# A transformer layer: shift rows turned by VectorE, row maxima made ten steps ahead

## The reference

```python
q = (x @ wq).reshape(B, S, 16, 16); k, v = (x @ wk), (x @ wv)   # 4 key/value heads
q = q * cos + rotate_half(q) * sin                              # the same for k
scores = einsum('bqkgd,bskd->bkgqs', q, k) / sqrt(16)
x = layernorm(x + einsum('bkgqs,bskd->bqkgd', softmax(scores), v) @ wo)
h = silu(x @ Wg.T) * (x @ Wu.T)                                 # W = (int - 128) * scale
x = layernorm(x + h @ Wd.T)
```

## Time and profile before

| | |
|---|---|
| median of 3 runs | 936.12 us (935.14 to 936.33) |
| span of the profiled execution, slowest core | 932.5 us |
| mean granted TensorE clock | 0.988 |
| busy: PE / DVE / ACT / POOL | 98% / 81% / 77% / 27% |
| share of the chain that ended last: PE | 92% |
| row_max transpositions (line 1186) | 32, median 277 ns |
| shift DMAs (line 363) | 128, median 634 ns |

### The profile page before, as it was taken

One profiled execution on the slowest core, in us unless ns is written; L12 is line 12 of the kernel. 1 busy time (PEld: TensorE's weight loads), 2 busy tenths in 40 slices (PEclk: granted clock), 3 DMA queues, 4 the chain that ended last, 5 costly groups with the idle time before them and its releaser, 6 DMA issues.

```text
span 932.5 us, 15773 instructions
## 1 busy us (share of the span) xinstructions
PE 914.6 (98%) x5574; PEld 465.6 (50%) x5574; DVE 753.7 (81%) x1519; ACT 715.2 (77%) x932; POOL 249.5 (27%) x214
## 2 busy tenths in 40 slices
PE   9998999999999999999999999999999999999996
PEld 3323434343443434434344344434335888888885
DVE  5777999999999999999999999999973456655555
ACT  2456898989889988889988989898896555555564
POOL 7752565010010001001000100400101666656455
PEclk9997999999999999999999999999999999999998
DMA  7986433222133132223313133221110201101001
GB/s 258 281 227 189 96 90 84 72 69 52 43 75 80 43 66 59 51 65 70 72 42 75 46 63 70 69 51 43 32 52 15 70 24 46 46 23 46 24 24 47
DMA packets 50080, 68.78 MB, mean 74 GB/s; under 512 B 13520, under 2 KB 23760, under 8 KB 50000
## 3 DMA queue, kind: packets, MB, share of 16 engines
q1 hardware_dynamic: 49136, 64.61, 26.9%
q0 software_dynamic: 864, 3.15, 1.1%
HBM read 46.74 MB, written 16.25 MB: 68 GB/s over the span
## 4 chain that ended last, share of the span: by engine, by line
PE 92%; DVE 3%; ACT 2%; issue 1%; DMA 1%; SPq 1%; POOL 0%; POOLq 0%; DVEq 0%; ACTq 0%
PE pv_bank L1266 27%; PE ring_bank L1173 26%; PE pair_bank L1324 13%; PE pair_bank L1387 11%; PE pv_bank L1413 3%; PE ring_bank L1413 3%; PE ring_bank L1276 2%; PE pair_bank L1214 2%; ACT probs L1087 1%; PE ring_bank L1186 1%; PE ring_bank L1291 1%; PE pv_bank L1155 1%; PE ring_bank L1229 0%; DMA q_parts<-low 0%; DVE by_sin L727 0%
## 5 line engine op out<-in xcount | busy, mean ns | idle before, releaser
L1087 ACT ACTIVATE probs<-pair_bank 128x1024 f32<-128x1024 f32 x512 | 496.4, 1026 | 68.8 <-PE pair_bank L1324 67.6
L762 DVE TENSOR_REDUCE block_max<-ring_bank 128x1 f32<-128x512 f32 x732 | 468.8, 682 | 31.6 <-PE ring_bank L1173 23.7
L1173 PE MATMUL ring_bank<-k_max,q_sb 48*128 48x512 f32 x1003 | 314.8, 475 | 3.6 <-ACT above L1032 1.4
L1266 PE MATMUL pv_bank<-probs,v_all 128*32 128x512 f32 x2048 | 273.5, 606 | 0.6 <-ACT probs L1087 0.5
L1173 PEld LDWEIGHTS ring_bank<-k_max,q_sb 48*128 48x128 f32 x1003 | 136.5, 184 | 251.9 <-DVE block_max L762 127.4
L1324 PE MATMUL pair_bank<-q_sb,k_sb 50*128 50x512 f32 x1024 | 204.9, 416 | 0.9 <-ACT probs L1087 0.7
L619 POOL TENSOR_TENSOR attn<-attn,inv_rows 128x1024 f32<-128x1024 f32 x7 | 16.7, 2384 | 491.4 <-DMA inv_rows<-inv_d 491.4
L1324 PEld LDWEIGHTS pair_bank<-q_sb,k_sb 50*128 50x128 f32 x1024 | 101.2, 186 | 33.6 <-ACT probs L1087 15.1
L944 DVE SCALAR_TENSOR_TENSOR hid<-pair_bank,up_s,silu 128x512 f32<-128x512 f32 x63 | 47.1, 747 | 84.7 <-ACT silu L1134 84.7
L667 POOL TENSOR_TENSOR hid_l<-hid,hid_h 128x512 fp32r<-128x512 f32 x63 | 81.8, 1298 | 86.0 <-ACT hid_h L1113 85.3
L759 DVE CUSTOM_DVE_ANT_0 above<-ring_bank,above 128x512 f32<-128x512 f32 x137 | 94.4, 691 | 12.5 <-ACT above L1032 5.2
(11 more groups left out here) (140 smaller groups left out, 860.6 us busy)
## 6 DMA issues: line engine op xcount, KB each, us to landing
k_max<-k_parts SPq DMA_DIRECT2D x96, 96.0 KB, 3.5
q_sb<-q_parts SPq DMA_DIRECT2D x64, 128.0 KB, 3.4
k_sb<-k_parts SPq DMA_DIRECT2D x96, 64.0 KB, 2.3
attn<-xT SPq DMA_DIRECT2D x8, 512.0 KB, 5.1
q_parts<-high SPq DMA_DIRECT2D x16, 256.0 KB, 3.8
q_parts<-low SPq DMA_DIRECT2D x16, 256.0 KB, 4.1
q_sb<-q_parts SPq DMA_DIRECT2D x64, 64.0 KB, 3.5
attn<-pv_sb SPq DMA_DIRECT2D x128, 32.0 KB
```

Of the source, the lines that this page charges most:

```text
L762: dve.reduce_max(block_max[half % 2][:, col:col + 1], bank, axis=AX.X).then_inc(ring_used, 1)
L1087: act.activation(probs[t % 2][:, 2 * pr:2 * pr + 2, :], pair_bank[pr][:], ACT.Exp, scale=D ** -0.5).then_inc(probs_ready, 1)
L1173: pe.matmul(bank, q_sb[k][rows, i, qt * P:(qt + 1) * P], k_max[k // QH][rows, kind * CH:(kind + 1) * CH], start=True, stop=True).then_inc( ...
L1266: ins = pe.matmul(pv_bank[32 * j:32 * j + 2 * D, :], v_all[:, head, t, :], probs[t % 2][:, 2 * (j % 2) + j // 2, :], start=(t == 0), stop= ...
```

## The change

The turn from columns to rows goes from TensorE to VectorE. `row_max` is rounded where it lies, as 128x16 (`shift_high`), then the remainder is taken (`shift_low`), both into `shift_rows`, 128 partitions by 32 columns. `turn_shift` transposes this in four squares of 32x32: after it, partition 32 b + 16 o + c of `shift` holds part o of column c for the 32 queries of block b. TensorE's transposition and its ring bank go away; the three instructions stand behind the second, third and fourth block of a step.

Since each row of `q_sb` is now spread over four squares, `load_shift` issues eight DMAs, one for each part and square, each with 16 pieces of 32 numbers. It waits for a semaphore of its own, `shift_ready`.

`LEAD` goes from 12 to 10, so a half's last maxima are made in step 5 of the half before instead of step 3, and the three instructions stand in step 6 (`HIGH_AT`). For half 0 they stand behind blocks 2, 3 and 6 of the second half's early blocks. In the last pair the output projection's first part (`OUT_AT` = 6) waits for the last maxima.

```diff
-LEAD = 12
-SPLIT_AT = 5
+LEAD = 10
+HIGH_AT = 6
+OUT_AT = 6
...
-        shift = [sb(f"shift{c}", [G * QT, SHIFT, P], f32r, two) for c in range(2)]
+        shift_rows = [sb(f"shift_rows{c}", [P, SHIFT, G * QT], f32r, two) for c in range(2)]
+        shift = [sb(f"shift{c}", [P, SQ], fp32, two) for c in range(2)]
...
-            def load_shift(pair, k, split):
-                sp.wait_ge(*split)
-                for r in range(GROUPS):
-                    heads = G // GROUPS * QT
-                    for o in range(SHIFT):
-                        row = r * GROUP + ROWS + o
-                        dst = q_sb[k][row:row + 1].rearrange("o j (q p) -> o (j q) p", p=P)
-                        sp.dma_start(dst.bitcast(fp32), shift[k % 2][r * heads:(r + 1) * heads, o, :].bitcast(fp32)).then_inc(shift_loaded[k], 16)
+            def load_shift(pair, k):
+                sp.wait_ge(shift_ready, HALVES * pair + k + 1)
+                for o in range(SHIFT):
+                    for b in range(P // SQ):
+                        dst = q_sb[k][ROWS + o::GROUP].rearrange("r j (q b p) -> r (j q) b p", q=QT, p=SQ)[:, :, b, :]
+                        src = shift[k % 2][b * SQ + o * G * QT:b * SQ + (o + 1) * G * QT]
+                        sp.dma_start(dst.bitcast(fp32), src).then_inc(shift_loaded[k], 16)
...
-            def split_shift(bank, half, index, guard):
-                if guard is not None:
-                    dve.wait_ge(*guard)
-                dve.tensor_copy(shift[half % 2][:, 0, :], bank[0:G * QT, 0:P]).then_inc(shift_h_ready, 1)
-                dve.wait_ge(shift_h_ready, index + 1)
-                dve.tensor_tensor(shift[half % 2][:, 1, :], bank[0:G * QT, 0:P], shift[half % 2][:, 0, :].bitcast(fp32), ALU.subtract).then_inc(ring_used, 1)
+            def shift_high(half):
+                dve.wait_ge(row_max_ready, half + 1)
+                dve.tensor_copy(shift_rows[half % 2][:, 0, :], row_max[half % 2][:]).then_inc(shift_h_ready, 1)
+
+            def shift_low(half):
+                dve.wait_ge(shift_h_ready, half + 1)
+                dve.tensor_tensor(shift_rows[half % 2][:, 1, :], row_max[half % 2][:], shift_rows[half % 2][:, 0, :].bitcast(fp32), ALU.subtract).then_inc(shift_l_ready, 1)
+
+            def turn_shift(half):
+                dve.wait_ge(shift_l_ready, half + 1)
+                if half > 1:
+                    dve.wait_ge(shift_loaded[(half - 2) % HALVES], SHIFTS * ((half - 2) // HALVES + 1))
+                dve.transpose(shift[half % 2][:], shift_rows[half % 2][:].rearrange("p o n -> p (o n)").bitcast(fp32)).then_inc(shift_ready, 1)
...
             def maxima(g):
+                turned = shift_at(g)
                 for e in range(4):
...
                     if maxima_at(g):
                         half, t = maxima_at(g)
                         take_max(half, 4 * t + e)
+                    if turned is not None and e:
+                        (shift_high, shift_low, turn_shift)[e - 1](turned)
...
-            def transpose_max(half):
-                pe.wait_ge(row_max_ready, half + 1)
-                bank = free_bank((half, "split"))
-                pe.transpose(bank[0:G * QT, 0:P], row_max[half % 2][:], ident[:]).then_inc(ring_ready, 1)
...
-                            if k == QH and t == SPLIT_AT + 1:
-                                pe.wait_ge(*taken_through((HALVES * PAIRS - 1, "split")))
-                            part = g - (KT * (HALVES * PAIRS - 2) + SPLIT_AT + 1)
+                            if k == QH and t == OUT_AT:
+                                pe.wait_ge(*taken_through((HALVES * PAIRS - 1, MAXES - 1)))
+                            part = g - (KT * (HALVES * PAIRS - 2) + OUT_AT)
```

More of the change, by code:

```diff
@@ L29 @@
 SHIFT = 2
-SHIFTS = 16 * GROUPS * SHIFT
+SQ = 32
+SHIFTS = 16 * SHIFT * P // SQ
 QT = CH // P
 MAXES = G * QT * QH
-RING = MAXES + 1
 BANKS = 3
-LEAD = 12
-SPLIT_AT = 5
+LEAD = 10
+HIGH_AT = 6
+OUT_AT = 6
 FIRST = 5
@@ L237, in layer @@
             where = early[(n, h) if n < BLOCKS else (BLOCKS, HOOKS - 1)]
-            if i == 2 * KT + 1:
-                where.append((0, "split"))
             where.extend(step(i))
@@ L246, in layer @@
                 for key in early[n, h]:
-                    place(key, key[0] if key[0] in ("v", "gap") else "max" if key[1] == "split" else ("above" if blocks(key[0], key[1] // 4)[key[1] % 4][1] == 2 else "max"))
+                    place(key, key[0] if key[0] in ("v", "gap") else ("above" if blocks(key[0], key[1] // 4)[key[1] % 4][1] == 2 else "max"))
         early_entries = len(readers)
@@ L253, in maxima_at, with shift_at @@
             return (half, t) if half < HALVES * PAIRS else None
-        def split_at(g):
+        def shift_at(g):
             n, t = divmod(g, KT)
-            return n + 1 if t == SPLIT_AT and n + 1 < HALVES * PAIRS else None
+            return n + 1 if t == HIGH_AT and n + 1 < HALVES * PAIRS else None
         for g in range(HALVES * PAIRS * KT):
             for e in range(4):
-                if e == 1 and split_at(g) is not None:
-                    place((split_at(g), "split"), "max")
                 if maxima_at(g):
@@ L409, in projections @@
                     if last and c == 1:
-                        load_shift(0, 0, taken_through((0, "split")))
+                        load_shift(0, 0)
                     store_q(m, 1)
@@ L489, in attention @@
                     if k < HALVES - 1:
-                        load_shift(p, k + 1, taken_through((n + 1, "split")))
+                        load_shift(p, k + 1)
                     elif not last:
-                        load_shift(p + 1, 0, taken_through((n + 1, "split")))
+                        load_shift(p + 1, 0)
                     if k % QH == 0 and not last:
@@ L797, in early_maxima @@
                         row_maxima(half)
+                    if half and e == 2:
+                        shift_high(0)
+                    if half and e == 3:
+                        shift_low(0)
+                    if half and e == 6:
+                        turn_shift(0)
             for m in range(BLOCKS):
@@ L819, in maxima @@
             def maxima(g):
+                turned = shift_at(g)
                 for e in range(4):
-                    if e == 1 and split_at(g) is not None:
-                        half = split_at(g)
-                        guard = None if half < 2 else (shift_loaded[(half - 2) % HALVES], SHIFTS * ((half - 2) // HALVES + 1))
-                        split_shift(entry((half, "split")), half, half, guard)
                     if maxima_at(g):
@@ L1039, in early_takes @@
                         gap_high(key[1])
-                    elif key[1] != "split" and key[1] % 4 < 2:
+                    elif key[1] % 4 < 2:
                         difference(key[0], key[1] // 4, (key[1] % 4,))
@@ L1201, in early_work @@
                         make_gap(key[1])
-                    elif key[1] == "split":
-                        transpose_max(key[0])
                     else:
@@ L1338, in attention @@
                         if t not in MIXED:
-                            if split_at(g) is not None:
-                                transpose_max(split_at(g))
                             maxima(1)
```

5 lines of the change are left out of this document (1 added, 4 removed).

## The result

The changed kernel takes 1116.68 us (median of 4 runs, 1115.07 to 1118.7). The kernel before, measured beside it, takes 935.63 us (4 runs, 933.85 to 936.33). The ratio is 1.192, 95% interval 1.1895 to 1.1946. Forecast was 1118 us in a range of 1040 to 1165.

A forecast was written before the change was run, and what follows sets the result against it. TensorE was taken as the bound, busy 914.6 of 932.5 us. 30 boundaries x (4.5 stand + 1.6 clock - 0.2 gain) = 177, with 1 + 1 + 3 at the ends +182, gave 1118 us, range 1040 to 1165.

The forecast's parts named there:

- Lead of 2.1 us: At each boundary between halves: VectorE's transposition ends 2.1 us before TensorE needs the shift rows, 0.2 put down for transposing.
- Latency of eight DMAs, 6.5 us: SyncE's shift DMAs: the last of eight begins 4.8 us after the first and lands 1.7 later; bounds 4.8 and 7.3.
- The stand: TensorE waiting for shift rows before step 0: 4.5 us at each of 30 boundaries, bounds 2.7 and 5.5.
- Clock, 1.6 us a half: Behind each of 30 stands: TensorE runs 3.4 us at the lower clock, losing 1.6 us; bounds 0 and 3.2.
- Gain of 0.2 by the transposition gone: Attention halves: TensorE's transposition and VectorE's PSUM copies go, three small instructions come; 0.2 us gained a half, bounds 0 and 0.3.
- Start and last boundary, +1 and +3: Attention's start hangs on half 0's shift, +1 us; the boundary into half 31 stands 2.6 us plus slow clock, +3.
- Time around the span, 3.6 us: Whole run: the median 936.12 us lies 3.6 above the profiled span of 932.5; the sum is added to both.
- the clock doesn't fall: Rival at the stands: the clock stays up or is back before it matters; 1070 us, chance 0.12.
- Cheap issue: Rival at the shift DMAs: issues 0.47 apart, 1.5 to land, stand 2.7 + 0.1; 1066 us with the clock, chance 0.11.
- Rows in time: Rival at the boundaries: all eight DMAs fit into the 2.1 us lead, TensorE never stands; 928 us, chance 0.03.
- what I named as signs: Profile: 30 waits of 4.5 us, eight issues in 5.4, halves 25 to 26, clock near 0.93, VectorE and ScalarE busy time unchanged.

The follow-up runs named there:

- e8: Changed kernel with each of the eight shift DMAs cut in two, one per destination row of q_sb: 1311.95 us, ratio 1.3999.
- e1: Changed kernel with 14 dummy matmuls on TensorE ahead of its wait for the shift rows, at 29 boundaries: 1046.49 us, ratio 1.1165.
- e3: Changed kernel with row maxima twelve steps ahead again and the turn in step 4, VectorE's transposition and eight DMAs kept: 930.16 us, ratio 0.9919.
- e6: e3 with half 0's transposition two blocks earlier, right behind its remainder: 929.94 us, ratio 0.9932.
- e9: e6 with rounding and remainder made by reductions over a single SBUF source instead of cast and subtraction: 929.74 us, ratio 0.9935.
- e4: Kernel before, TensorE's transposition and four DMAs kept, with maxima ten steps ahead and the transposition in step 6: 954.62 us, ratio 1.0177.
- e2: Changed kernel issuing only the rounded part's four DMAs from the second head pair on, leaving out part of the shift: 1008.14 us, ratio 1.0764.
- e7: Changed kernel with the remainder's four DMAs issued on ScalarE's queue beside SyncE's four: 1063.27 us, ratio 1.1369.
- e5: Changed kernel with rounding, remainder and transposition ahead of step 6's first block instead of behind its second to fourth: 1037.40 us, ratio 1.107.

## Why the prediction was right, and where its terms were off

The steps, in the prediction's order:

- *Lead of 2.1 us.* Right: 2.07. VectorE's transposition takes 0.20, as put down.
- *Latency of eight DMAs, 6.5 us, by 7 x 0.68 + 1.7.* Too long by 1.03: 5.47. The step that failed is "I take 6.5, since source, destination and queue are those of the row". Issues are 0.55 apart, not 0.68; the last begins 3.9 us after the first, and TensorE goes on 1.6 later. Source and destination weren't the same: the row's DMAs wrote one row of `q_sb` from 8 partitions, the new ones two from 16. e8 shows that this counts, by going back to the former and to 632 ns. The stand is thus 3.43 where I took 4.5, inside the bounds of 2.7 and 5.5.
- *Clock, 1.6 us a half, from 3.4 us at the lower level.* Too small. The level lasts 211.6 us over 32 stretches, 6.6 on the mean, twice the row. A half is 25.58 where e1, which differs in the filling alone, has 23.21, and 22.85 where nothing disturbs it: 2.4 to 2.7 us a half. The bound of 3.2 held. The price put on each microsecond of it was too high in turn: 3.4 us were to lose 1.6, 0.47 each, and the 205 us that the filling took away lost 70, 0.34 each. Some 7 of the 205 us fell into stands, where they cost nothing.
- *The two errors cancel.* 4.5 + 1.6 = 6.1 a half was forecast; 25.58 - 19.47 (e3) = 6.1 came, of which 3.4 are stand and 2.7 come with the clock. That the total is right within 2 us is luck: the two errors were of one size with opposite signs. The mechanism was right, its two sizes were not.
- *Gain of 0.2 by the transposition gone.* It is 0.32 a half (e3: 19.47 against 19.79), and in the whole 7.4 us by the medians (937.52 to 930.16), some lost to VectorE instructions that GpSimd held. The section on the kernel before has GpSimd off this path; for the kernel before that is so, and for the changed one it isn't.
- *Start and last boundary, +1 and +3.* The start is 3.2 us later. One reason is that VectorE's cast at 75.92 took 0.73 us beside GpSimd's instruction, the other that the rows were turned at 78.07 and not near 75.3: the blocks that the three instructions stand behind end later than I read them. The last boundary stands for 1.95, less than the 2.6 assumed. The cast for half 1, at 101.58, was held for 2.30 us; TensorE then stood for 1.32, and the clock fell at 105.08. This is the one stretch of the 32 without a boundary, and no term had it.
- *Time around the span, 3.6 us.* It is 1.8 (1118.7 against 1116.9 for the same execution); 3.6 came from a median and the span of another execution. The sum was added to both alike, so nothing moves.

Put together from the runs: clock 70 us (after less e1), the stand and what goes with it 116 (e1 less e3), the turn itself -7 (e3 less before). These add up to the 179 us between the changed kernel and the 937.52 of the kernel before by construction; the check is in the halves, where 22.85 (e1, undisturbed) less 19.47 (e3) is 3.38, the length of the stand. Over 30 boundaries that is 101 us; seven held turns of e1, 1.0 to 2.0 us each, make about 9 more.

The rivals: "the clock doesn't fall" gave 1070, and e1 is that case by construction, 1046. "Cheap issue" was half true: 0.55 lies between its 0.47 and my 0.68; its 1066 needed the small clock term too. "Rows in time" would have needed a latency of 2.1 us; with four DMAs it is still 3.29. Most of what I named as signs came: a wait of TensorE for q_sb<-shift at every boundary, eight issues in a row from 2 us before it runs dry, halves of 25.6, busy time of VectorE and ScalarE nearly unchanged. Three were off in size, and each belongs to a mis-sized term: the waits were of 3.4 us and not 4.5, the eight issues took 4.4 us and not 5.4, and the clock fell further than 0.93, to 0.892.

## What to carry to other kernels

Before moving work later, write down the slack at the wait that ends it (here 6.37 us from data to need, of which four DMAs used 3.8) and charge it with every change of the same edit: by the boundary each of these two fits it by itself, both together overdraw it by 3.4 us thirty times. For a small copy that is waited for, count the DMAs, since the issues are in series: here they made 3.9 of 5.5 us, and an issue took 495 or 632 ns by the form of the DMA and not by the size of its pieces. And price a repeated stand of TensorE at well over its length: here 3.4 us of stand cost another 2.4 to 2.7 in clock, and filling the stand with dummy products took that back.

## What the runs showed of the hardware

- *VectorE held by GpSimd.* In the changed kernel, e3 and e6 together, 20 of VectorE's small SBUF-to-SBUF casts and subtractions begin inside a GpSimd instruction; 19 of them end 0.02 to 0.04 us behind its end, after 0.17 to 2.3 us, where the median is 164 to 171 ns; the last ends earlier and still took 0.97. The cast and subtraction of the kernel before read PSUM; five begin inside a GpSimd instruction, and all 64 take 269 to 279 ns. One-source reductions (e9) aren't held either. The Trainium skill (SBUF — State Buffer, SBUF: two separate sides) says that VectorE and GpSimd share a pair of ports as an exclusive lock, held for a whole instruction, and that VectorE needs it in its two-port modes or with two SBUF inputs. These 19 agree with it, and so does e4, where all 21 that begin inside a GpSimd instruction read PSUM and take 278 to 280 ns. Not all cases agree with "a whole instruction": in GpSimd's conversion of the weights (w_f<-w_raw, 2.77 us) three of them were let go 1.71 us before its end (changed kernel, e2, e7), and two of e7 that began 1.34 and 2.05 us into it took 0.17. So by moving the source from PSUM to SBUF the change made an operation shorter and exposed it at once.
- *The clock after short stands.* In the changed kernel stands of 3.3 us came with the lower level at each boundary; stands of 2.1 us did in 22 of 31 (e7), of 1.2 in 16 of 28 (e5) and 6 of 26 (e2). The changed kernel's falls come between 1.6 us before work is back and 1.8 us after, and last 3.4, 6.8 or 10.2 us. The Trainium skill (TensorE: Matmul & The Clock Gate, HAM oscillation — how this bites in real kernels) describes a loop whose every turn waits for a DMA and then starts slow. The trace of the changed kernel agrees in that the loss comes back at each of the 31 boundaries; but at most of them work starts at the full clock and slows up to 1.8 us later.
- *Two queues issuing at once* slow each other, 703 and 586 ns for 495 (e7).
